# Half-precision scores for the softmax maximum from batch 3 on, and a reordered end of attention

## What is computed

```
q = layernorm(x) @ Wq;  k = ctx @ Wk;  v = ctx @ Wv        # 16 heads of 32
q, k = rope(q), rope(k)
attn = softmax(q @ k.T / sqrt(32))                           # 120 keys
x = x + (attn @ v) @ Wo
h = act_qdq(layernorm(x))                                    # one scale, max |h| over everything
up, gate = act_qdq(h @ Wup.T), act_qdq(h @ Wgate.T)          # weights dequantized from 4 bits
o = act_qdq(act_qdq(gate * u16(sigmoid(gate))) * up)
out = x + o @ Wdown.T
```

## Time and profile before

| | us |
|---|---|
| median of 3 runs | 2352.8 |
| lowest, highest | 2349.05, 2352.96 |
| the profiled execution | 2357.08 |
| its span, first to last instruction | 2355.3 |
| granted clock, mean | 0.982 |
| PE busy | 2244.6 (95%) |
| DVE busy | 1679.3 (71%) |
| ACT busy | 1283.8 (55%) |
| POOL busy | 702.0 (30%) |

### The profile page before, as it was taken

How to read it: one execution, slowest core, us unless ns; L and a number is a source line. 1 busy time by engine, 2 the same in 40 slices (tenths; PEclk the granted TensorE clock), 3 DMA queues, 4 the chain that set the end, 5 groups by cost and what they waited for, 6 DMA issues and landing times. The chain is left out here.

```text
span 2355.3 us, 32497 instructions
## 1 busy us (share of the span) xinstructions
PE 2244.6 (95%) x12869; PEld 1011.3 (43%) x12869; DVE 1679.3 (71%) x1700; ACT 1283.8 (55%) x1195; POOL 702.0 (30%) x658
## 2 busy tenths in 40 slices
PE   5898999999998899999999999999999599999999
PEld 3443434444443344444444444444444244444444
DVE  7556778888875757545543398888888887777774
ACT  3335554545443223222322588878877677777772
POOL 3354565665654321000100064444444000000000
PEclk9899999999999999999999999999999899999999
DMA  6333677786778567788876699777777466555552
GB/s 191 92 104 109 162 160 185 161 192 160 188 160 170 129 189 251 259 251 266 255 245 197 229 351 320 287 283 279 286 288 293 177 232 232 219 209 208 215 221 89
DMA packets 286715, 500.22 MB, mean 212 GB/s; under 512 B 187500, under 2 KB 189804, under 8 KB 249692
## 3 DMA queue, kind: packets, MB, share of 16 engines
q1 hardware_dynamic: 286556, 498.09, 67.1%
HBM read 247.75 MB, written 186.58 MB: 184 GB/s over the span
## 5 line engine op out<-in xcount | busy, mean ns | idle before, releaser
L1623 PE MATMUL banks<-XB,W 128*128 128x512 f16 x2304 | 500.3, 381 | 2.3 <-ACT XB L1649 2.3
L1623 PE MATMUL banks<-XB,WT 128*128 128x512 f16 x2304 | 497.4, 379 | 0.0
L2089 PE MATMUL banks<-W,OH 128*128 128x512 f16 x2256 | 487.1, 379 | 3.5 <-DVE OH L2191 3.5
L1643 ACT ACTIVATE OB<-banks,uns 128x512 f32<-128x512 f32 x384 | 255.1, 683 | 387.3 <-PE banks L1623 384.6
L1623 PEld LDWEIGHTS banks<-XB,W 128*128 128x128 f16 x2304 | 225.7, 98 | 276.5 <-issue 5.2
L1623 PEld LDWEIGHTS banks<-XB,WT 128*128 128x128 f16 x2304 | 225.1, 98 | 272.2
L2089 PEld LDWEIGHTS banks<-W,OH 128*128 128x128 f16 x2256 | 220.4, 98 | 270.2 <-DVE OH L2191 4.0
L1910 POOL TENSOR_TENSOR PR<-GS,OB 128x2048 f32<-128x2048 f32 x46 | 220.5, 4793 | 257.6 <-ACT OB L1643 247.7
L1732 DVE TENSOR_REDUCE amx<-OB 128x1 f32<-128x2048 f32 x48 | 109.7, 2286 | 237.5 <-ACT OB L1643 237.5
L932 ACT ACTIVATE P<-banks 120x2048 f32<-120x2048 f32 x60 | 112.4, 1873 | 176.4 <-PE banks L653 176.4
L1273 DVE TENSOR_REDUCE MX<-banks 128x16 f32<-128x1920 f32 x64 | 138.0, 2156 | 72.8 <-PE banks L689 72.8
(11 more groups left out here) (266 smaller groups left out, 2925.4 us busy)
## 6 DMA issues: line engine op xcount, KB each, us to landing
g_s<-OB SPq DMA_DIRECT2D x48, 1024.0 KB, 6.5
GL<-g_s SPq DMA_DIRECT2D x48, 1024.0 KB, 7.5
up_s<-OB SPq DMA_DIRECT2D x48, 1024.0 KB, 4.9
XA<-up_s SPq DMA_DIRECT2D x32, 1024.0 KB, 9.4
gq_s<-GQ SPq DMA_DIRECT2D x48, 512.0 KB, 4.8
XD<-gq_s SPq DMA_DIRECT2D x48, 512.0 KB, 6.7
XA<-in_x SPq DMA_DIRECT2D x16, 1024.0 KB, 7.1
QW<-QE SPq DMA_DIRECT2D x128, 128.0 KB, 2.5
```

The source lines that it names most:

```text
L1623: t = e.matmul(pk[:].rearrange("p (j t) -> p j t", j=4), WT[w][:, ot, wa, kk, :], XB[i % 2][:, xa, :, kk, :], start=(kk == 0 and wa == 0 a ...
L1643: e.activation(OB[n % 3][:, r, :], bank[(k + 4) % 8][:], ACT.Copy, scale=uns[:, 12 * w + ot:12 * w + ot + 1]).then_inc(s_ev, 1)
L2089: t = e.matmul(pk[:].rearrange("p (r n) -> p r n", r=4), OH[i % 2][:, a, ot, j * 128:(j + 1) * 128], WD[:, :, c, wa, o4, :], start=(ot == ...
```

## The change

From unit 12 on (`HALF`, batch 3), ACT makes half-precision copies of the rotated queries and keys of a unit, scaled by 1/QS each (`act_half`): the queries go into the unit's QE buffer, which POOL and the swap have finished with, the keys into two small buffers KH. `pe_largest` reads these copies and waits for them. ACT may overwrite QE only when the largest that reads it is done (`act_rope_in`), and SP may load x into QE near the end only then. The scale of MT takes the factor back.

At the end of attention: DVE instead of POOL normalizes units 58 and 59 and subtracts for unit 59; it does the scaling of the second batch of XA later; SP issues the reciprocals' loads of units 56 to 59 before the x1 store and x load that preceded them, and the last two gate transposes after the store of row group 60; for row group 63 DVE does sums and aggregate before largest and smallest. Some semaphores are merged or split for this.

```diff
+HALF = 12
+        KH = [W0[:, 12000 + SK * i:12000 + SK * (i + 1)] for i in range(2)]
+        def qh(u):
+            return QE[ROT["q", u] % 2][:].bitcast(FP16)[:, 0:512]
@@ sp_xr_load, row groups LATE and LATE + 1
                 e.wait_ge(s_qw[1], 32 * (len(ROTS) // 2))
+                e.wait_ge(s_sm, NU - 1 + u - LATE)
@@ sp_gate_turn
+            if t == NO - 1:
+                e.wait_ge(s_sm, NU)
@@ sp_attention, after the steps
             dma_recip_out(e, B - 2)
+            for u in range(NU - 8, NU - 4):
+                dma_recip(e, u)
             sp_x1_out(e, LATE + 3)
             sp_xr_load(e, LATE + 6)
-            for u in range(NU - 8, NU - 4):
-                dma_recip(e, u)
-            sp_gate_turn(e, NO - 2)
-            sp_gate_turn(e, NO - 1)
             for u in range(LATE + 4, NU):
                 sp_x1_out(e, u)
                 if u + 3 < NU:
                     sp_xr_load(e, u + 3)
+                if u == NU - 4:
+                    sp_gate_turn(e, NO - 2)
+                    sp_gate_turn(e, NO - 1)
@@ pe_largest
+            if u >= HALF:
+                e.wait_ge(s_half, u - HALF + 1)
+                q_, k_ = qh(u), KH[u % 2]
+            else:
+                q_, k_ = QR[u % 8], KR[g0][:, c, bb * SK:(bb + 1) * SK]
             for j in range(4):
                 for g in range(4):
-                    t = e.matmul(PB[:, g, j * SK:(j + 1) * SK], QR[u % 8][32 * g:32 * g + 32, j * 128:(j + 1) * 128],
-                                 KR[g0][32 * g:32 * g + 32, c, bb * SK:(bb + 1) * SK], start=True, stop=True)
+                    t = e.matmul(PB[:, g, j * SK:(j + 1) * SK], q_[32 * g:32 * g + 32, j * 128:(j + 1) * 128],
+                                 k_[32 * g:32 * g + 32, :], start=True, stop=True)
@@ pe_output
             if u >= NU - 4:
-                e.wait_ge(s_alo, u + 1)
+                e.wait_ge(s_alo, u)
+            elif u == NU - 8:
+                e.wait_ge(s_alo, NU - 5)
+                e.wait_ge(s_dn, 3)
@@ act_rope_in
+                what, u = ROTS[before]
+                if what == "q" and u >= HALF:
+                    e.wait_ge(s_sm, u + 1)
+
+        def act_half(e, u):
+
+            g0, bb = divmod(u // 4, 4)
+            n = ROT["q", u]
+            e.wait_ge(s_radd, n + 1)
+            e.wait_ge(s_rm1, n + 1)
+            e.wait_ge(s_qw[n % 2], 32 * (n // 2 + 1))
+            if u >= HALF + 2:
+                e.wait_ge(s_sm, u - 1)
+            e.activation(KH[u % 2], KR[g0][:, u % 4, bb * SK:(bb + 1) * SK], ACT.Copy, scale=1.0 / QS)
+            e.activation(qh(u), QR[u % 8][:], ACT.Copy, scale=1.0 / QS).then_inc(s_half, 1)
@@ act_attention, in step s, after the QE copy of unit s
+                if HALF <= s - 1 < NU:
+                    act_half(e, s - 1)
@@ dve_attention, the end
             row_group(NU - 10)
+            dve_normal_unit(e, NU - 6)
+            dve_normal_unit(e, NU - 5)
+            dve_x1(e, NU - 9)
+            u = NU - 5
+            e.wait_ge(s_ah, u + 1)
+            e.tensor_tensor(AH[0][:, 1, 3, :], A[:, u % 6, :], AH[0][:, 0, 3, :], ALU.subtract).then_inc(s_dn, 1)
+            dve_x1_stats(e, NU - 9)
+            dve_x1_aggregate(e, B - 3)
             dve_normal(e, 1)
-            row_group(NU - 9)
-            dve_x1_aggregate(e, B - 3)
             dve_x1(e, NU - 8)
...
-            for u in range(NU - 4, NU):
+            for u in range(NU - 4, NU - 1):
                 row_group(u)
+            dve_x1(e, NU - 1)
+            dve_x1_sums(e, NU - 1)
             dve_x1_aggregate(e, B - 1)
+            dve_x1_range(e, NU - 1)
@@ pool_attention, the end
             pool_low(e, NU - 8)
-            pool_normal(e, NU - 6)
             pool_low(e, NU - 7)
-            pool_normal(e, NU - 5)
             pool_low(e, NU - 6)
-            pool_low(e, NU - 5)
```

More of the change, by code:

```diff
@@ L157, in build @@
         s_xt = sem("s_xt")
-        s_qsc = sem("s_qsc")
+        s_half = sem("s_half")
         s_k = sem("s_k")
@@ L184, in build @@
         s_rb = sems("s_rb", 4)
-        s_rt = sem("s_rt")
         s_re = sem("s_re")
@@ L188, in build @@
         s_an = sem("s_an")
+        s_dn = sem("s_dn")
         s_ah = sem("s_ah")
@@ L754, in pe_recip @@
             elif j >= 2:
-                e.wait_ge(s_an, NU - 4 + j - 1)
+                e.wait_ge(s_dn, 3 + j - 1)
             for c in range(4):
@@ L825, in pe_attention @@
                 t = e.transpose(BS_[:, j * 128:(j + 1) * 128], RC[:, j * 128:(j + 1) * 128], id32[:])
-            t.then_inc(s_rt, 1)
+            t.then_inc(s_tx, 1)
             pe_output(e, NU - 7)
@@ L834, in pe_attention @@
                 pe_output(e, u)
-            e.wait_ge(s_an, NU)
+            e.wait_ge(s_dn, 7)
             e.wait_ge(s_g, 1)
@@ L907, in act_largest @@
                 e.wait_ge(s_c1, 4 * (b - 1) + 4)
-            e.activation(MT[:], BQ_, ACT.Copy, scale=1.0 / MS).then_inc(s_mte, 1)
+            e.activation(MT[:], BQ_, ACT.Copy, scale=(QS * QS if 4 * b >= HALF else 1.0) / MS).then_inc(s_mte, 1)
         def act_attention(e):
@@ L950, in act_attention @@
                     if s == 0:
-                        e.wait_ge(s_qsc, 1)
+                        e.wait_ge(s_sel, 3)
                     act_rope_in(e, n)
                     e.activation(QE[n % 2][:], BQ_, ACT.Copy, scale=qsc[:]).then_inc(s_qe, 1)
+                if HALF <= s - 1 < NU:
+                    act_half(e, s - 1)
                 if s == 1:
@@ L1006, in act_attention @@
             for u in range(NU - 8, NU - 4):
-                e.wait_ge(s_an, u + 1)
+                if u < NU - 6:
+                    e.wait_ge(s_an, u + 1)
+                else:
+                    e.wait_ge(s_dn, u - NU + 7)
                 e.wait_ge(s_o, NU - 12)
@@ L1020, in act_attention @@
             for j in range(4):
-                e.wait_ge(s_an, NU - 4 + j + 1)
+                e.wait_ge(s_dn, 3 + j + 1)
                 e.wait_ge(s_o, NU - 8)
@@ L1141, in dve_x1_stats, with dve_x1_sums @@
         def dve_x1_stats(e, u):
+            dve_x1_sums(e, u)
+            dve_x1_range(e, u)
+        def dve_x1_sums(e, u):
             ob, j = divmod(u, 4)
@@ L1147, in dve_x1_stats, with dve_x1_range @@
             e.bn_stats(st2[:, ob % 2, j, :], x1).then_inc(s_st2, 1)
+        def dve_x1_range(e, u):
+            _, x1, _, _ = x_of(u)
+            e.wait_ge(s_x1, u + 1)
             e.tensor_reduce(xmx[:, u:u + 1], x1, AX.X, ALU.max).then_inc(s_st2, 1)
@@ L1165, in dve_last, with dve_normal_unit @@
             e.scalar_tensor_tensor(part, part, vun[:, 1:2], bank[6 + j % 2].rearrange("p (c t) -> p c t", c=4),
-                                   ALU.mult, ALU.mult).then_inc(s_an, 1)
+                                   ALU.mult, ALU.mult).then_inc(s_dn, 1)
+        def dve_normal_unit(e, u):
+            to, sem_, n = rb(u)
+            e.wait_ge(sem_, n)
+            e.wait_ge(s_a, u + 1)
+            e.tensor_tensor(A[:, u % 6, :], A[:, u % 6, :], to, ALU.mult).then_inc(s_dn, 1)
         def dve_v_max(e, g):
@@ L1219, in dve_attention @@
             e.wait_ge(s_wsc, 3)
-            e.tensor_scalar(qsc[:], wsc[:, 1, 2:3], 1.0 / XS, None, ALU.mult).then_inc(s_qsc, 1)
+            e.tensor_scalar(qsc[:], wsc[:, 1, 2:3], 1.0 / XS, None, ALU.mult).then_inc(s_sel, 1)
             dve_x_low(e, 0)
@@ L1334, in dve_attention @@
             row_group(NU - 10)
+            dve_normal_unit(e, NU - 6)
[6 more added lines that the diff above has]
+            dve_x1_aggregate(e, B - 3)
             dve_normal(e, 1)
-            row_group(NU - 9)
-            dve_x1_aggregate(e, B - 3)
             dve_x1(e, NU - 8)
-            e.wait_ge(s_rt, 1)
+            e.wait_ge(s_tx, 2)
             e.wait_ge(s_rd, 16 * (B - 1))
@@ L1353, in dve_attention @@
             dve_x1_aggregate(e, B - 2)
-            for u in range(NU - 4, NU):
+            for u in range(NU - 4, NU - 1):
                 row_group(u)
+            dve_x1(e, NU - 1)
+            dve_x1_sums(e, NU - 1)
             dve_x1_aggregate(e, B - 1)
+            dve_x1_range(e, NU - 1)
             e.wait_ge(s_rs2, 2 * B)
+            e.wait_ge(s_st2, 3 * NU)
             e.tensor_tensor(xmx[:], xmx[:], mv2[:, :, 0], ALU.subtract).then_inc(s_da, 1)
```

## The result

The changed kernel takes 2340.16 us (median of 5 runs, 2335.49 to 2341.92), against 2352.96 us before in the same session: a ratio of 0.9945, 95% interval 0.9933 to 0.9957, or 12.8 us faster. The forecast was 2350.6 within 2339 to 2359. So the time lies inside the range, but only 1 us above its low end; the forecast's own terms gave -2.2 us, its own narrower range began at 2346, and its largest chance (0.45) was on no measurable change.

What follows compares the result with a forecast made beforehand. Two loops were taken to bound the batches, TensorE's of 39.68 us and a second of 39.06. Terms of -1.1 us in the batches and -1.1 at the end gave -2.2, so 2350.6 us, range 2339 to 2359.

Steps and rivals of the forecast that it cites:

- The two loops: Per batch: TensorE's, 39.68 us; second, T0 (largest awaiting ACT's exponential, c=1) through QE, SP, POOL, DVE, ACT to T0, 39.06.
- Rival (a) wholly: Regular batches: TensorE is the bound after all, the second loop shortens with it; 33 us off, 2320; chance 0.07.
- The largest, taken as 0.5: Units 12 to 63 on TensorE: 0.5 us instead of 1.10, between bounds of 0.33 and 1.10; 2.4 saved per batch.
- The gain per batch, taken as 0.10: Regular batches: second loop's slack of 0.47 us, less 0.37 for the later QE copy; 1.1 us over 11 batches.
- The half copies on ACT, taken as free: Copies of queries and keys behind the QE copy: some 0.9 us per unit, costing nothing while ACT's idle covers them.
- The lower clock behind the longer wait, taken as absorbed: Output after TensorE's long wait at T0: 1.7 us slower, within 3 us of new room per batch, costing nothing.
- The end, -1.1 forecast: End of attention: +0.8 for SP's load, -0.6 for the move to DVE, -1.3 for the aggregate; -1.1 us together.
- SP's load into QE, +0.8: Step 64: the load waits for the largest of unit 62, delaying reciprocals and the output: +0.8 us (0 to +1.5).
- The move to DVE, -0.6: Before the output of unit 56: POOL's 3.6 us become 3.0 on DVE, between 2.4 and 4.2; -0.6 us.
- The aggregate before largest and smallest, -1.3: Last row group: DVE's 1.40 us wait for POOL is filled with two reductions moved under it; -1.3 us.
- The gate transposes, 0: Last two moved between the last x1 outputs: 0, at most +2 us if a late x1 store holds DVE's last scale.
- rival (a) in part: Regular batches: those with no slack, long by a late DMA, go; 6 to 12 us off, about 2343; chance 0.20.

Runs made afterwards that it cites:

- e4: Kernel before, with SP issuing the transpose of x a step later, behind the swap and the load of x, from step 15 on: 2344.31 us, ratio 0.9962.
- e6: Changed kernel, with the half-precision largest of units with c = 3, the one at T0, done four times over: 2350.69 us, ratio 0.9993 to the kernel before.
- e10: Kernel before, with only the wait of the QE copy for the largest added, the largest staying in float32: 2357.98 us, ratio 1.0018.
- e1: Kernel before, with only the changes of the end; largest in float32 throughout, two SP waits on it left out: 2345.91 us, ratio 0.9969.
- e2: Kernel before, with only the half-precision largest, its copies and waits; the end in its old order: 2347.38 us, ratio 0.9972.
- e7: Changed kernel, with the last reciprocals' loads put back behind the x1 store and the x load: 2345.12 us, ratio 0.9964 to the kernel before.
- e8: Changed kernel, with the two normalizations and the subtraction left on POOL: 2344.49 us, ratio 0.9967 to the kernel before.
- e3: Changed kernel, with SP issuing the transpose of x a step later from step 15 on: 2324.94 us, ratio 0.9872 to the kernel before.

## Why the range held, and where the prediction's steps failed

**The two loops: right in the main.** The period is set mostly by the second loop, through the QE copy, SP, POOL, DVE and ACT. Of the 27.6 us by which PE's busy time fell, 17.9 turned into waiting (2.85 to 2.99 us at T0 in most batches); the forecast had nearly all of it. Rival (a) wholly, periods of 37 to 38 with PE gapless, didn't come. e4, e6 and e10 show the loop from three sides. What the forecast didn't have is a second way from TensorE into it, by the QE copy of c = 0 and POOL's cosine.

**The largest, taken as 0.5: it is 0.32.** It runs like the lower bound, four groups of 512 columns in 0.33. The Trainium skill prices a weight load at columns/1.2, 107 ns here ("TensorE: Matmul & The Clock Gate", section "LDWEIGHTS (loading the stationary operand)"); the row of loads above has 93 ns, near it. But sixteen loads of 93 ns and their matmuls go through in 0.32 us, so loads of different row groups go side by side, and sixteen in series are not what one pays. With that the QE copy starts at +0.52, not +0.60.

**The gain per batch, taken as 0.10 (0.47 of slack less 0.37): mis-sized, and this is the step that failed.** Measured are 0.52. I read how long DVE's reduce at c = 0 waits for TensorE, and called that all the slack. But the second loop meets TensorE at two places: the reduce at c = 3 waits for it as well. Two such rows of DVE before:

```profile
279.38 2.16 DVE L1273 TENSOR_REDUCE MX<-banks 128x16 f32<-128x1920 f32 x1 [0.16 <-PE banks L689]
...
363.37 2.16 DVE L1273 TENSOR_REDUCE MX<-banks 128x16 f32<-128x1920 f32 x1 [1.51 <-PE banks L689]
```

In the eleven batches it waits in six: 1.07, 0.16, 1.51, 0.38, 0.25 and 0.23, 3.6 us in all, 0.33 per batch. It is tempting to add up: 0.47 + 0.33, less the copy's delay of 0.29, gives 0.51. That sum was made after the result, and its parts don't hold. Here are the averages of a batch, over the 30 batches of the three profiles with a float32 largest and the 50 of the five with the half-precision one:

| from | to | float32, us | half, us |
|---|---|---|---|
| T0 | the next swap | 13.73 | 13.74 |
| swap | reduce at c = 3 | 7.82 | 7.17 |
| reduce at c = 3 | reduce at c = 0 | 9.66 | 9.67 |
| reduce at c = 0 | next T0 | 9.13 | 9.24 |

The whole gain lies before the reduce at c = 3, the place that I had left out: 0.33 of the 0.65 are its wait for TensorE, and the sine in front of it comes 0.28 us earlier, for which I have no cause. The slack at c = 0, the only one in the forecast, brought nothing: the wait for TensorE (0.45 per batch) is gone, but DVE's scaling is held by POOL for 0.36 us per batch instead of 0.12, and DVE waits for the load of x for 0.36 instead of 0.21, so its run from c = 3 on is not unbroken in every batch, as the prediction had it. The delay of the QE copy isn't seen at the next swap, though e10's of 1.08 is. And from the reduce at c = 0 to T0 it takes 0.10 more. That the gain of a batch comes in before c = 3 is shown; why the freed wait at c = 0 is filled so exactly is argued from these rows and was not tested by a run.

**The half copies on ACT, taken as free: nearly.** They take 0.62 and 0.30 us and stand behind the QE copy. The 0.10 us per batch between the reduce at c = 0 and T0 (9.24 against 9.13), 1 us in all, stand in no term; the cause is open.

**The lower clock behind the longer wait, taken as absorbed: not shown.** 4.2 to 4.45 us for 2.76 in seven of the eleven batches. In the profile of the result six of the ten periods after batch 3's have it and last 38.48 to 40.48 us, the other four 38.75 to 39.25; the step from 38.75 to 40.43 above is the longer output come through to the period. Over the fifty batches it is 40.0 us with it and 39.7 without; with their spread that can't be told from nothing. So on average most of it may be absorbed, but not in every batch.

**The end, -1.1 forecast: -5.2 measured in the trace.**
- SP's load into QE, +0.8: not seen. From the last T0 to the output of unit 52 it is 99.7 and 100.1 us after, 101.2 and 99.6 before. But with TensorE's longer wait before it that output itself takes 1.7 us more, at the lower clock, and that was in no term.
- The move to DVE, -0.6: from the output of unit 52 to that of unit 56 it is 28.10 and 27.74 us before, 26.29 and 26.30 after. The later two hold the 1.7 us of the item above; like with like, the move and the reciprocals' loads together are worth 2.7 to 3.2 us (25.07 in e1 against before, 29.44 in e2 against after). The step that failed here is that I costed the move and left out the other edit beside it, though the diff shows it: SP issues the loads right behind the reciprocals' store. They went out 3.69 us after that store began before (x1 store and x load lay between), and 1.53 us after it now. Either edit undone costs 2.4 to 2.5 us (e7, e8). The DVE normalization beside POOL took 1.42 us against 0.69 alone, as the earlier trace rows had it. The Trainium skill ("SBUF — State Buffer", section "Who interferes with whom") says that such a DVE instruction and GpSimd share one port pair by a lock; this row agrees. Most of these 0.7 us stands on the path, behind the wait for the loads: from the start of that normalization to the output it is 777.94 - 774.80 = 3.1 us, about the 3.0 that I took and not the 4.2 of the upper end. For the scaling at c = 0 in the batches the forecast had no such term.
- The clock of the output of unit 56, not in the sum: 5.27 to 2.75, -2.5 us. With the gap cut from 4.11 to 0.62 the lower clock didn't come. I had seen this pattern in the regular batches, and failed to read it in the earlier trace rows, where the 5.27 stood.
- The aggregate before largest and smallest, -1.3: PE's wait for the scale is 4.78 instead of 5.83, -1.05. Right. The gate transposes, 0: nothing of them is seen.

That the time lies in the range is in good part luck. The range reached down for rival (a) in part ("batches go that are long by a late transfer"), and that didn't happen: periods above 41 us are 7 of 30 with the float32 largest and still 7 of 50 with the half-precision one, the longest 42.6 in both. The gain came from the reduce at c = 3 and from the end.

## What to carry to other kernels

When two loops share a program, look for the waits of the second for the first at every place where they meet, not only at the last one, and don't take a wait for a gain: another engine can fill it, as POOL did here. Before costing an edit that relieves the busiest engine, look for the queue item that stands in the second loop: here one 8 us transpose issue before a swap was worth 8.6 us by itself and 15 us on top of the change, more than the relief of TensorE (5.5 us alone). And at a lone gap on the path, count the slower clock behind the gap as part of its price.

## What the runs showed that I had not expected

- Sixteen f16 matmuls of 32 rows, 128 x 120, with their loads take 0.32 us; thirty-two in f32 took 1.10. That is a third and not a half.
- The issue of the x transpose holds SP's queue for 8.0 to 8.9 us in the ten batches after and for 7.0 to 8.5 a step later (e3, e4). Its place decides who waits.
- The clock after a gap is not told by the gap's length alone: twelve matmuls take 4.44 us after a gap of 3.16 (unit 52, e2) and 2.75 after 3.18 (unit 56, e8).
- A short DVE instruction can cost five times its length: the scaling of 128 x 64 takes 0.25 us alone and up to 1.37 beside POOL's multiplication, in 30 of the 50 batches with the half-precision largest at least 0.68.
- Batch periods of one and the same code spread by 6 us over ten batches from profile to profile (396.2 to 402.2) as soon as no TensorE floor cuts them off; with the floor by 1.4 (402.8 to 404.2). A gain of 5 us there can't be read from one pair of profiles.
